# Text attention in units of one block, with a stacked update and spare matmuls, and the second attention's keys and values in the first stage

## The reference, cut

```python
# first layer: text attention (bitnet_linear: ternary weights, activations rounded to int8 by one global maximum)
image_embeds = bitnet_linear(bitnet_linear(dinov2_features, W_d2v, b_d2v), W_img, b_img)
fused = bitnet_linear(text_embeddings, W_txt, b_txt)            # 1024 x 256 per batch
for Wa, ba in ((W_att0, b_att0), (W_att1, b_att1)):
    kv = bitnet_linear(image_embeds, Wa, ba)                    # 64 x 128 per batch
    k = jnp.concatenate([kv, kv], axis=-1)
    scores = jnp.einsum('bse,bpe->bsp', fused, k) * inv_sqrt_e
    attn = jax.nn.softmax(scores, axis=-1)
    fused = fused + 0.1 * jnp.einsum('bsp,bpe->bse', attn, k)
# second layer: masked cross attention
q = xn @ Wq
kv = context @ Wkv                                              # 128 x 192 by 192 x 2048
k, v = jnp.split(kv, 2, axis=-1)
```

## Time and profile before

| what | us |
|---|---|
| median of 3 runs | 1418.81 (1414.84 to 1419.8) |
| the profiled execution | 1425.58 |
| its span in the trace | 1423.6 |
| TensorE busy | 1112.4 (78%) |
| VectorE busy | 988.6 (69%) |
| ScalarE busy | 475.3 (33%) |
| GpSimd busy | 395.4 (28%) |

### The profile page before, as it was taken

How to read it: one execution, slowest core, us unless ns; L and a number is a source line. 1 busy time by engine, 2 the same in 40 slices (tenths; PEclk the granted TensorE clock), 3 DMA queues, 4 the chain that set the end, 5 groups by cost and what they waited for, 6 DMA issues and landing times. The chain is left out here.

```text
span 1423.6 us, 20621 instructions
## 1 busy us (share of the span) xinstructions
PE 1112.4 (78%) x6831; PEld 926.3 (65%) x6832; DVE 988.6 (69%) x1802; ACT 475.3 (33%) x1058; POOL 395.4 (28%) x541
## 2 busy tenths in 40 slices
PE   1488888667586879999822489898988999898987
PEld 0277777655165659888711268787777778687877
DVE  7699999555856102222249999999999999999610
ACT  0111111001063043232200155555555464555453
POOL 1112222100013400000040043625445353536353
PEclk9999999866778579999966789999999999999999
DMA  6035600000000836666353000000000000000000
GB/s 225 15 115 194 235 12 4 1 0 0 1 1 32 351 112 221 248 216 232 142 220 134 0 1 1 1 7 0 7 0 7 0 7 0 0 8 0 9 8 9
DMA packets 23972, 98.86 MB, mean 69 GB/s; under 512 B 3728, under 2 KB 15184, under 8 KB 17584
## 3 DMA queue, kind: packets, MB, share of 16 engines
q1 hardware_dynamic: 16080, 72.13, 13.5%
q10 hardware_dynamic: 5200, 18.85, 4.0%
q0 software_dynamic: 2640, 7.21, 1.5%
HBM read 87.96 MB, written 21.76 MB: 77 GB/s over the span
## 5 line engine op out<-in xcount | busy, mean ns | idle before, releaser
L1850 PE MATMUL bank<-n_hA_hi_reduced,ffn_h 128*128 128x256 f32 x512 | 129.2, 294 | 14.7 <-POOL n_hA_lo_reduced L1677 14.2
L1850 PE MATMUL bank<-n_hB_hi_reduced,ffn_h 128*128 128x256 f32 x512 | 125.8, 290 | 6.1 <-ACT n_hA_lo L1976 4.4
L1850 PE MATMUL bank<-n_hA_lo_reduced,ffn_h 128*128 128x256 f32 x512 | 125.5, 287 | 0.0
L1850 PE MATMUL bank<-n_hB_lo_reduced,ffn_h 128*128 128x256 f32 x512 | 120.3, 279 | 0.0
L1850 PEld LDWEIGHTS bank<-n_hA_hi_reduced,ffn_h 128*128 128x128 f32 x512 | 101.1, 197 | 18.4 <-POOL n_hA_lo_reduced L1677 17.0
L2088 DVE TENSOR_TENSOR d_prod<-d_qk,d_xT 128x512 f32<-128x512 f32 x128 | 104.5, 856 | 0.6
L1850 PEld LDWEIGHTS bank<-n_hB_hi_reduced,ffn_h 128*128 128x128 f32 x512 | 96.5, 189 | 9.4 <-ACT n_hA_lo L1976 5.8
L1850 PEld LDWEIGHTS bank<-n_hA_lo_reduced,ffn_h 128*128 128x128 f32 x512 | 101.3, 198 | 0.2
L1850 PEld LDWEIGHTS bank<-n_hB_lo_reduced,ffn_h 128*128 128x128 f32 x512 | 96.6, 189 | 1.8 <-issue 1.7
L1511 DVE TENSOR_TENSOR e_y<-bank,e_b 128x256 f32<-128x256 f32 x23 | 9.8, 424 | 124.0 <-PE bank L1441 124.0
L1486 ACT ACTIVATE e_hT<-bank,e_b 128x128 f32<-128x128 f32 x184 | 52.4, 368 | 127.2 <-PE bank L1429 127.2
(11 more groups left out here) (327 smaller groups left out, 2687.3 us busy)
## 6 DMA issues: line engine op xcount, KB each, us to landing
e_w<-in_W SPq DMA_DIRECT2D x23, 1024.0 KB
ffn_weights<-in_F ACTq DMA_DIRECT2D x2, 5632.0 KB, 20.0
e_piece<-ffn_weights SPq DMA_DIRECT2D x11, 1024.0 KB, 4.8
ffn_h<-ffn_weights SPq DMA_DIRECT2D x2, 4096.0 KB, 18.8
ffn_w<-ffn_weights SPq DMA_DIRECT2D x3, 1024.0 KB, 6.9
expert_rows<-zero ACTq DMA_DIRECT2D x1, 2944.0 KB, 11.6
e_xs<-expert_rows SPq DMA_DIRECT2D x23, 128.0 KB, 4.5
expert_out<-e_y POOLq DMA_DIRECT2D x23, 128.0 KB, 2.0
```

The source lines that it names most:

```text
L1850: last = nc.tensor.matmul(F[f % 2][:, 0:PAIR], weight(w[:, k, f * P:(f + 1) * P], fast), operand(src[part][1][:, k, :], fast), start=(c == ...
```

## The change

The arithmetic of the text attention is written differently. Since the key is `kv` twice, a score is the sum of both feature halves times `kv`: the quantised input is projected with the sum of the two weight halves (`q_txt_sum`, bias `b_txt_sum`), and one matmul per 128 tokens gives the scores of both layers (`kvT` now has both layers side by side). The second layer's scores lack the first update, which is added as the first probabilities times `cross01` = 0.2 `kv0` `kv1` (L974). Both layers' probabilities are stacked on 128 rows (`pT`) and give one update matmul, added once (L996). The loop is unrolled over the four blocks u, which overlap; every block has buffers of its own. ScalarE takes the projections out of PSUM. TensorE gets 108 spare matmuls (L852), whose result nobody reads.

The second attention's keys and values are computed in `stage_bits` (L320), as matmuls of 96 rows; `Wkv` (1.5 MB) is loaded there before f1, no longer in `stage_attn0`, and a copy of the context goes through ScalarE's queue. They wait in the last parts of `cross_M` and `cross_N`.

```diff
@@ stage_bits
+                if name == "f1":
+                    for c in range(KD):
+                        rows = slice(c * HALF_DC, (c + 1) * HALF_DC)
+                        sp.dma_start(wkv[0:HALF_DC, c, :], ins["wkv"][rows, :]).then_inc(wkv_loaded, 16)
...
+            pe.wait_ge(cxx_loaded, 32)
+            pe.wait_ge(wkv_loaded, 32)
+            keys_or_values(0)
             summed(1)
             pe.wait_ge(kvT_ready, 1)
...
+            last.then_inc(products_done, 1)
+            keys_or_values(1)
...
+            nc.vector.tensor_tensor(m.q_txt_sum[:, :, :], q_txt[:, :, 0:P], q_txt[:, :, P:2 * P], ALU.add)
+            nc.vector.tensor_tensor(m.b_txt_sum[:, :], m.bcol[:, 4:5], m.bcol[:, 5:6], ALU.add)
...
-            link(nc.vector.tensor_copy(m.kv[:, :, :, :].rearrange("p l b c -> p (l b c)"), ps_t[0:SC, :]))
+            v.wait_ge(products_done, 1)
+            link(nc.vector.tensor_copy(m.kv[:, :, :].rearrange("p b c -> p (b c)"), ps_t[:, 0:B * P]))
+            link(nc.vector.tensor_scalar(m.cross01[:, :, :].rearrange("p b s -> p (b s)"),
+                                         ps_t[0:SC, B * P:B * P + B * SC], 0.2, None, ALU.mult))
@@ stage_mix, TensorE
+            def spare(n):
+
+                for _ in range(n):
+                    nc.tensor.matmul(bank_w[:, 0:256], m.identb[:, :], m.maskb[:, 0:4, :].rearrange("p t s -> p (t s)"),
+                                     start=True, stop=True)
+
+            spare(8)
             pe.wait_ge(amax_ready, 1)
...
+            spare(12)
+            for u in range(2):
+                projected(u, 0)
+                projected(u, 1)
+                scores(u)
+                projected(u, 2)
+            spare(4)
+            turned(0, 0)
...
+            spare(8)
+            turned(3, 1)
+            spare(8)
+            updates(3)
@@ stage_mix, VectorE
+            def quantised(u):
+                part = m.xT[:, :, where(u)[1]]
+                link(V.tensor_scalar(part, part, col[:, 2:3], MAGIC, ALU.mult, ALU.add))
+                V.tensor_scalar(m.qx[:, :, where(u)[1]], part, MAGIC, 127.0, ALU.subtract, ALU.min).then_inc(qx_ready, 1)
+
+            def shifted(u, l):
+                if l:
+                    v.wait_ge(second_done[u], 1)
+                    v.wait_ge(kept, u + 1)
+                    link(V.tensor_tensor(pr[u][:, :, :], sa[u][:, :, :], second_of(u), ALU.add))
+                    from_ = pr[u][:, :, :]
+                else:
+                    v.wait_ge(score_done, u + 1)
+                    from_ = scores_of(u, 0)
...
+                if not l:
+                    V.tensor_copy(sa[u][:, :, :], scores_of(u, 1)).then_inc(kept, 1)
...
+            quantised(0)
+            quantised(1)
+            shifted(0, 0)
+            quantised(2)
+            shifted(1, 0)
+            probabilities(0, 0)
+            quantised(3)
+            probabilities(1, 0)
+            shifted(2, 0)
+            shifted(0, 1)
+            probabilities(2, 0)
+            shifted(1, 1)
+            probabilities(0, 1)
+            shifted(2, 1)
+            probabilities(1, 1)
+            shifted(3, 0)
+            updated(0)
+            probabilities(3, 0)
+            probabilities(2, 1)
+            updated(1)
+            shifted(3, 1)
+            updated(2)
+            probabilities(3, 1)
+            updated(3)
@@ stage_route
-            sp.wait_ge(kvx_done, 2)
             sp.wait_ge(slot_ready, 1)
...
-            pe.wait_ge(m.raws_loaded, 16 * 4)
-            pe.wait_ge(ctx_loaded, 32)
-            keys_or_values(0)
             pe.wait_ge(hot_ready, 1)
...
-            keys_or_values(1)
+            pe.wait_ge(m.raws_loaded, 16 * 2)
```

More of the change, by code:

```diff
@@ L287, in quantised, with keys_or_values @@
                 last.then_inc(mm_done, 1)
+            def keys_or_values(n):
+                for f in range(KF):
+                    c = f % 4 * P
+                    for k in range(KD):
+                        last = nc.tensor.matmul(G[2 * n + f // 4][:, c:c + P],
+                                                wkv[0:HALF_DC, k, n * FF + f * P:n * FF + (f + 1) * P],
+                                                x_ctx[0:HALF_DC, k, :], start=(k == 0), stop=(k == KD - 1))
+                last.then_inc(kvx_done, 1)
             pe.wait_ge(consts_ready, 1)
@@ new lines, in stage_mix, with where @@
+    tx = [s(f"b_tx{u}", [P, KD, BLK], F32) for u in range(NU)]
+    ts = [s(f"b_ts{u}", [P, BLK], F32) for u in range(NU)]
+    pr = [s(f"b_pr{u}", [P, TQ, SC], F32) for u in range(NU)]
+    sa = [s(f"b_sa{u}", [P, TQ, SC], F32) for u in range(NU)]
+    text, score, bank_p, bank_g, bank_w, upd = m.banks[0:2], m.banks[2:4], *m.banks[4:8]
+    kept = sem("b_kept")
+    TURNS = [(0, 0), (1, 0), (2, 0), (0, 1), (1, 1), (3, 0), (2, 1), (3, 1)]
+    def where(u):
+        return u % B, bass.ds(u // B * BLK + u % B * S, BLK)
@@ new lines, in projected @@
+            def projected(u, g):
+                n = 3 * u + g
+                if g == 0:
+                    pe.wait_ge(qx_ready, u + 1)
+                if n >= 2:
+                    pe.wait_ge(text_read, n - 1)
+                for k in range(KD):
+                    w = m.q_txt_sum[:, k, :] if g == 0 else m.q["txt"][:, k, (g - 1) * P:g * P]
+                    last = nc.tensor.matmul(text[n % 2][:, :], w, m.qx[:, k, where(u)[1]],
+                                            start=(k == 0), stop=(k == KD - 1))
+                last.then_inc(text_done, 1)
@@ new lines, in scores @@
+            def scores(u):
+                pe.wait_ge(text_read, 3 * u + 1)
+                if u >= 2:
+                    pe.wait_ge(sub_ready[u - 2], 1)
+                    pe.wait_ge(kept, u - 1)
+                for t in range(TQ):
+                    last = nc.tensor.matmul(score[u % 2][:, t * P:(t + 1) * P], ts[u][:, t * P:(t + 1) * P],
+                                            m.kvT[:, u % B, :, :].rearrange("p l s -> p (l s)"), start=True, stop=True)
+                last.then_inc(score_done, 1)
@@ new lines, in turned, with second @@
+            def turned(u, l):
+                n = TURNS.index((u, l))
+                pe.wait_ge(prob_ready[u], l + 1)
+                if n:
+                    pe.wait_ge(probT_ready, n)
+                for t in range(TQ):
+                    last = nc.tensor.matmul(bank_p[l * SC:(l + 1) * SC, t * P:(t + 1) * P], pr[u][:, t, :], m.ident[:, :],
+                                            start=True, stop=True)
+                last.then_inc(prob_turned, 1)
+            def second(u):
+                pe.wait_ge(probT_ready, TURNS.index((u, 0)) + 1)
+                if u:
+                    pe.wait_ge(sub_ready[u - 1], 2)
+                for t in range(TQ):
+                    last = nc.tensor.matmul(bank_g[:, t * SC:(t + 1) * SC], pT[u][0:SC, t * P:(t + 1) * P],
+                                            m.cross01[:, u % B, :], start=True, stop=True)
+                last.then_inc(second_done[u], 1)
@@ new lines, in _ @@
+            spare(4)
+            second(0)
+            spare(4)
+            turned(1, 0)
+            projected(3, 0)
+            projected(3, 1)
+            spare(4)
+            second(1)
+            projected(3, 2)
+            scores(3)
+            spare(4)
+            turned(2, 0)
+            spare(4)
+            turned(0, 1)
+            spare(4)
+            second(2)
+            spare(4)
+            updates(0)
+            spare(4)
+            turned(1, 1)
+            spare(4)
@@ L788, in _ @@
+            projected(2, 1)
+            projected(2, 2)
+            exped(2, 0)
+            copied(1, 0)
+            projected(3, 0)
+            exped(0, 1)
+            projected(3, 1)
+            projected(3, 2)
+            copied(2, 0)
+            exped(1, 1)
+            copied(0, 1)
+            exped(2, 1)
+            exped(3, 0)
+            copied(1, 1)
+            copied(3, 0)
+            copied(2, 1)
+            exped(3, 1)
+            copied(3, 1)
         @block.vector
@@ L1232, in _ @@
         def _(pe):
-            def keys_or_values(n):
-                for f in range(KF):
-                    c = f % 4 * P
-                    for k, rows in ((0, P), (1, DC - P)):
-                        last = nc.tensor.matmul(G[2 * n + f // 4][:, c:c + P],
-                                                m.wkv[0:rows, k, n * FF + f * P:n * FF + (f + 1) * P],
-                                                cx[0:rows, k, :], start=(k == 0), stop=(k == 1))
-                last.then_inc(kvx_done, 1)
             def folded_queries(b):
```

253 lines of the change are left out of this document (120 added, 133 removed).

## The result

The changed kernel takes **1392.58 us** in the median of 4 runs (1390.33 to 1393.19), the kernel before 1416.82 (4 runs on the same chip): a ratio of 0.9825, 95% interval 0.9806 to 0.9843. It is 24 us faster, inside the range, and 13.6 us slower than the forecast of 1379.

What follows compares the result with a forecast made beforehand. Stages run one after another: handovers bound text attention, TensorE the routing, VectorE the first stage. 0.5 - 19.1 - 21.1 = -39.7 takes the profiled 1425.6 to 1385.9, less 6.8 to the median: 1379 us, range 1366 to 1399.

Steps and rivals of the forecast that it cites:

- Text attention: Text attention stage: bounded by no engine, a chain of handovers; 55 us instead of 74.1, so -19.1.
- the walk: Text attention: four engine queues followed in new program order; end at 50.8 us at full clock, 76.8 at half clock.
- Rival A: Text attention: the clock stays low, the stage takes 77 us instead of 55, the kernel 1401; chance 0.10.
- First stage: First stage, bounded by VectorE: keys and values added there cost +0.5 us, between 0 and +4.7.
- ScalarE's additional DMA issues and copies lie in idle time: First stage: ScalarE's added issues and copies cost 0, at most 1 us either way.
- My upper end: First stage: keys at their present slow pace end at 37.7, 4.2 us late for VectorE; kernel 1383, inside the forecast's 0.47.
- Routing: Routing stage, its end set by TensorE: earlier ranks and folding end it at 500.0 instead of 521.07, -21.1 us.
- I keep the 6.6 us: Routing: the stall of 6.6 us, taken as slow supply of instructions while transfers fill the queues, stays.
- Rival B: Routing: the stall does not recur, 6.6 us less, kernel 1372; chance 0.20.
- land by about 490, before the experts need them: Routing: `W2` and first `W1`, 10 MB, take 26 us at 388 GB/s; with biases and scatter, in by about 490.
- C: Routing: a longer stall, folding starved until the transfers drain; stage ends at 510.7, kernel 1390; chance 0.20.
- D: Text attention: the unrolled queue is not supplied in time, 103 us more, kernel 1501; chance 0.03.

Runs made afterwards that it cites:

- its twin: The kernels with both new loads moved and with half of `W2` loaded earlier besides have identical text attention code, which took 57.5 and 60.6 us.
- Before again: The unchanged kernel before, profiled in a second execution: 1415.89 us over 1416.94, ratio 0.9992, span 1413.1 us.
- early `W2`: Against the changed kernel with `Wkv` and the context's copy moved later: first four experts' `W2` loaded at the feed-forward's start; 1378.74 us over 1414.06.
- later maxima: Against the kernel with half of `W2` loaded earlier: first two blocks' maxima later, third update behind the last probabilities; 1373.47 us over 1417.29.
- both moved: Against the changed kernel: context's copy behind the small tables on ScalarE's queue, `Wkv` behind f1 and f2; 1386.60 us over 1416.94.

## Why the prediction was right and where it was off

**Text attention, right.** Forecast 55 for VectorE's own rows, between 51 and 77, measured 54.9. That it is so near is in part luck: six traces with this code have 56.3 to 60.7 us with the barrier (mean clock 0.92 to 0.86), and the profiled execution is at the short end. VectorE waited 19.8 us, so its own work is 35.1, against 35.4; the walk had 15.3 us of waits at full clock and 4 more for the clock, 19.3. It put the longest waits behind L838's third block and at the second and the last update, at 3.4, 3.6 and 2.9 us; the trace has 3.95, 4.03 and 4.34. The wait behind the eight spares at the start was put at 1.2 and is 1.94. The clock rose 4 us into the stage, as taken from the earlier trace rows; it was at half for less of the last 20 us than the third that I had allowed (0.82 on the last 11 us, 1.00 before). ScalarE's projections took 0.775 us, where the walk had 0.59. These two errors went against each other. Rival A, the low clock, did not come. Of the spares the prediction said that they cost 3.6 us of queue and "must earn it by the clock"; without them the stage was 1.5 us longer and the kernel's ratio the same (0.9828 against 0.9825), so they do no more than that.

On the two rules of the Trainium skill weighed there, "TensorE: Matmul & The Clock Gate", Part 1 (sustained activity releases the throttle) and HAM oscillation (waits between bursts re-throttle): each shows here in part. The dense start rose as the first has it, but TensorE was also busy 6.00 of 6.00 us with the folding from 454 to 460 and stayed at 0.50, as in the earlier trace rows: there the row decides. Where TensorE waited for VectorE the clock fell in one kernel and not in its twin, so the second rule says what may happen and not what will.

**First stage, the step that failed.** "ScalarE's additional DMA issues and copies lie in idle time", and so were put at 0. ScalarE is idle there, and that was the wrong resource: the queue that it issues to is an order, and what stands behind the new issues is the small tables that VectorE scales by. I had checked whether f1, the large transfer, stays ahead of VectorE (it did: its magnitude at 34.47 has no wait) and whether the keys end in time (they took 6.7 us against the 6.0 of the estimate, out at 41.75; the sum ran at 42.15, 7.68 us after the start of f1's magnitude, where it had been 33.53 - 25.84 = 7.69 before). Both of those terms were right. The stage lost 8.3 us all the same (6.3 of it the wait for `sc`, 3.5 in waits for raw weights, less 1.5 for the context), outside the +4.7 that I had allowed, 7.2 of it with the context's place. My upper end came from the one rival I could think of, a slow pace of the keys, and not from the other issues on the queue.

**Routing, right in direction, wrong in two sizes.** The rank matmul ran 0.29 us after the routing choice began and TensorE's folding started at 448.1. But two things stood in my sum that were not so. The first: "I keep the 6.6 us" of stall. Before again shows that it was in one execution and that its price was 10 us: the folding of the keys took 24.3 us there and 14.3 in the second execution, and the prediction had priced only the idle time in it (10.6 - 4.04). The reason given, a slow supply of instructions, has no support in the traces (section on before again). Rival B had no stall, which was right, and the time wrong, as a bound took its place. The second: the transfers "land by about 490, before the experts need them", reckoned as 26 us for `W2` and `W1`. The next stage's first transfer needs the scattered rows, which share the queues with all 13.7 MB; from 444.5 to 484 us these moved at 347 GB/s on average, and `e_xs` went out 8.6 us after the last engine had finished. (That it waited for the scatter's landing is read from the code; no row names it.) The early `W2` took 6 us of that away. Against the ordinary execution of the kernel before the gain was 14.5 us, not 21.1.

**The sum.** In the frame of the profiled executions the steps made -39.7 and 1385.9; 1392.19 was profiled, 6.3 more (6.5 by the rounded stages): +8.0 in the first stage, -3.4 in the routing (63.4 to 38.9, -24.5 instead of -21.1, since the whole stall went), -2.6 in the feed-forward, +3.4 in the experts, +1.1 elsewhere. I then took 6.8 us off, for the distance of before's profiled execution to its median. That distance was most likely the stall, which the three other traces of that stretch of code lack. The changed kernel has none to lack: its wait for transfers is the same in every trace (38.6 to 39.1 us of routing where `W2` was not moved), and its profiled execution is within 0.4 us of its median. The other half of the error is this subtraction.

Of the rivals, C had a time close to the measured (1390) by another cause: a starved folding, which the trace doesn't show. D did not come: the straight queue of the text attention was supplied. What remains open is why the clock was lower in the experts' first tiles after the change (188.0 us against 184.8; TensorE busy 4.86 of 5 us from 495 to 500 at a clock of 0.66). Without spares, and with the early `W2`, the stage took 184.9 and 184.6, and with the later maxima 188.7; I did not isolate a cause.

## What to carry to other kernels

A transfer added at the head of a queue is priced by what stands behind it there, small tables first, and by when those are read, not by whether the issuing engine is idle. When work leaves the engine that closes a stage, work out when the stage's transfers and the last scatter land by the stage's whole volume at its measured rate, since that is the next bound. And an odd slow stretch of a single profiled execution is first looked for in a second one, and enters a sum at most once.

## What the runs showed of the hardware

- A table of 16 KB that was issued 1.65 us later landed 12 us later, 18.0 us from its issue instead of 7.5, with a large transfer issued in between. Over thirteen traces: 5.9 to 7.5 us where it was issued ahead of the first large piece, 14.3 to 18.0 behind it.
- While the two pieces of `Wkv`, 96 rows each, moved, the queues were busy (share 1.0) at 237 to 251 GB/s (rows below); with the pieces of 128 rows they moved 410 to 435. With `Wkv` behind f1 and f2 the low rate moved with it, from 11 to 18 us to about 18 to 25:

```profile
11.00:18.00 7.00, 0.88 (x5) 0.79 (x6) 4.28 (x15) 0.00 (x0) 0.00 (x0) 1.00 1.08 237
20.00:23.00 3.00, 0.00 (x0) 0.00 (x0) 0.00 (x0) 0.00 (x0) 0.00 (x0) 1.00 0.99 420
```

(the changed kernel), and

```profile
20.00:23.00 3.00, 0.61 (x4) 0.34 (x4) 2.76 (x9) 0.00 (x0) 0.00 (x0) 1.00 1.00 251
```

(both moved). No experiment changed the number of rows. But the kernel before loads the same `Wkv` in the linear attention as a piece of 128 rows and one of 64, in one queue, and while the one and then the other moves the rate halves at the same busy share:

```profile
79.00:81.00 2.00, 2.00 (x16) 2.00 (x15) 1.93 (x3) 0.00 (x0) 0.00 (x0) 1.00 0.95 401
82.00:84.00 2.00, 2.00 (x16) 1.92 (x15) 1.17 (x5) 0.00 (x0) 1.18 (x2) 1.00 0.96 201
```

The second execution of before has 406 and 209 there. So the pieces with fewer rows moved slower in this case; how much of the first stage's loss is due to the 96 rows, no run isolates.
- A stall of the matmul queue, 16 instructions in 10.6 us, that lengthened the routing by 10 us in one execution and shows in none of the twelve other traces, of which three run the same code there. No transfer of instructions is recorded during it. Its cause stays open.
- In the folding, TensorE was busy for every microsecond from 448 to 460 and had half clock throughout, with tiles of 64 rows and 64 columns. Tiles of 64 x 256 followed from 461.9, and the clock rose from 464 on:

```profile
462.00:464.00 2.00, 2.00 (x10) 1.22 (x12) 0.00 (x0) 1.09 (x2) 1.70 (x2) 0.50 1.70 555
464.00:466.00 2.00, 1.56 (x12) 0.74 (x9) 0.00 (x0) 1.27 (x3) 1.39 (x3) 0.89 0.13 33
```
